# A transformer layer pair on one core: normalized context by way of memory, maxima folded into the queries, and a new order

## What is computed

```python
# layer 0: keys and values are the first 112 context rows
Q, K, V = relu(x @ Wq.T + bq), relu(c @ Wk.T + bk), relu(c @ Wv.T + bv)
out = softmax(causal_and_key_mask(Q @ K.T / 4)) @ V          # per head
x = gamma * norm(out * query_mask + x) + beta
# layer 1
q, k, v = split(layernorm(x) @ sa_wqkv)
r = x + merge(softmax(causal(q @ k.T / 16)) @ v) @ sa_wproj
k2, v2 = split(layernorm(ctx) @ ed_wkv)                      # all 375 rows
r = r + merge(softmax((layernorm(r) @ ed_wq) @ k2.T / 16) @ v2) @ ed_wproj
result = r + relu(layernorm(x) @ ff_w1) @ ff_w2
```

## Time and profile before

| | |
|---|---|
| median of 3 runs | 367.59 us (367.25 to 367.86) |
| profiled execution, its own time | 367.8 us |
| its span | 366.1 us |
| granted TensorE clock | 0.999 of full |
| DMA | 14.12 MB in 5300 packets |

### The profile page before, as it was taken

How to read it: one execution, slowest core, us unless ns; L and a number is a source line. 1 busy time by engine, 2 the same in 40 slices (tenths; PEclk the granted TensorE clock), 3 DMA queues, 4 the chain that set the end, 5 groups by cost and what they waited for, 6 DMA issues and landing times.

```text
span 366.1 us, 9692 instructions
## 1 busy us (share of the span) xinstructions
PE 348.3 (95%) x4144; PEld 262.9 (72%) x4144; DVE 224.6 (61%) x563; ACT 170.9 (47%) x299; POOL 52.2 (14%) x67
## 2 busy tenths in 40 slices
PE   8988999999999999999999999999999999999996
PEld 4656788777965678876876776766987768675674
DVE  4789998436668746567945758556944464264412
ACT  2267652650664255673444062763453643614350
POOL 2023331041022010122100041130100031000000
PEclk9999999999999999999999999999999999999999
DMA  7759202000000002000000200000000000000000
GB/s 200 218 192 376 69 23 92 2 2 0 27 0 2 2 7 81 27 14 15 3 2 8 79 2 14 2 2 14 1 4 0 2 2 2 15 2 13 4 2 25
DMA packets 5300, 14.12 MB, mean 39 GB/s; under 512 B 689, under 2 KB 2982, under 8 KB 5002
## 3 DMA queue, kind: packets, MB, share of 16 engines
q1 hardware_dynamic: 4970, 13.42, 11.1%
q10 hardware_dynamic: 288, 0.09, 0.1%
HBM read 12.59 MB, written 0.92 MB: 37 GB/s over the span
## 4 chain that ended last, share of the span: by engine, by line
PE 76%; DVE 13%; DMA 5%; ACT 2%; issue 2%; SPq 1%; POOL 0%; DVEq 0%
PE ring L501 35%; PE ring L743 8%; PE acc L647 8%; PE ring L757 5%; PE ring L622 5%; DVE negmax L1031 4%; PE ring L602 4%; PE ring L596 3%; DMA xh<-in_keys 3%; PE ring L634 2%; DVE negmax L1010 2%; PE ring L666 2%; PE ring L614 2%; DMA w_qk<-in_w_qk 1%; PE ring L708 1%
## 5 line engine op out<-in xcount | busy, mean ns | idle before, releaser
L1031 DVE TENSOR_REDUCE negmax<-ring 112x2 f32<-112x750 f32 x64 | 57.0, 936 | 23.7 <-PE ring L743 23.0
L856 ACT ACTIVATE exps<-ring 125x896 f32<-125x896 f32 x48 | 41.4, 914 | 39.5 <-PE ring L757 39.2
L1248 POOL TENSOR_SCALAR_AFFINE_SELECT exps<-exps 112x896 f32<-112x896 f32 x32 | 30.8, 987 | 118.9 <-ACT exps L856 118.9
L1010 DVE TENSOR_REDUCE negmax<-ring 112x8 f32<-112x896 f32 x32 | 33.4, 1085 | 22.1 <-PE ring L602 22.0
L743 PE MATMUL ring<-k,q 32*112 32x376 f32 x256 | 38.5, 518 | 1.2 <-ACT exps L856 0.5
L647 PE MATMUL acc<-exps,v 125*17 125x112 f32 (+1 forms) x1280 | 38.9, 261 | 0.2
L647 PEld LDWEIGHTS acc<-exps,v 125*17 125x17 f32 (+1 forms) x1280 | 28.1, 97 | 12.9 <-issue 10.3
L856 ACT ACTIVATE exps<-ring,pad 112x896 f32<-112x896 f32 x32 | 30.5, 1004 | 10.7 <-PE ring L634 10.6
L501 PE MATMUL ring<-w_b,h 128*112 128x256 f32 x128 | 29.3, 382 | 0.0
L501 PEld LDWEIGHTS ring<-w_b,h 128*112 128x112 f32 x128 | 22.1, 177 | 5.8 <-issue 1.1
L501 PE MATMUL ring<-n,w_b 128*128 128x224 f32 x128 | 25.7, 357 | 0.2
(11 more groups left out here) (139 smaller groups left out, 547.2 us busy)
## 6 DMA issues: line engine op xcount, KB each, us to landing
c_nat<-in_ctx SPq DMA_DIRECT2D x4, 750.0 KB
w_b<-in_w_b SPq DMA_DIRECT2D x1, 2304.0 KB, 13.4
xk_t<-in_xk_t SPq DMA_DIRECT2D x8, 224.0 KB, 4.6
w_a<-in_w_a SPq DMA_DIRECT2D x1, 1280.0 KB, 6.0
xh<-in_keys SPq DMA_DIRECT2D x4, 224.0 KB, 4.1
x_nat<-in_x SPq DMA_DIRECT2D x4, 224.0 KB, 3.3
out<-x SPq DMA_DIRECT2D x8, 112.0 KB, 1.8
rows_sb<-in_row SPq DMA_DIRECT2D x1, 560.0 KB, 7.8
```

The costliest lines, as they stand in the source:

```text
L856: return nc.scalar.activation(exps[0:k, EXP_AT[job], :, :], o[0:k, :, 0:4 * T], ACT.Exp, bias=bias)
L1010: v_max[b].step(nc.vector.tensor_reduce(negmax[0][:, slot(g, b), 2 * m_:2 * m_ + 2, :], o[0:T, :, 0:4 * T].rearrange("p r (j t) -> p r j t ...
L1031: x_max[b].step(nc.vector.tensor_reduce(negmax[1][:, b, 2 * m_:2 * m_ + 2, i], o[0:T, :, 0:S], AX.X, ALU.max, negate=True), g, 2 * i + m_ + 1)
L1248: p_masked[b].step(nc.gpsimd.affine_select(e, e, [[0, 8], [1, T]], ALU.is_ge, 0.0, base=0, channel_multiplier=-1), g, k)
```

## The change

Three things. First, the context comes a second time with features on partitions (`c_feat`); the numbers of each token (deviation and shift, `c_norm`) are written to memory and read back as rows spread over 128 partitions (`c_rows`); GpSimd multiplies and adds. ScalarE's normalizing and TensorE's transposes go. Second, keys too are kept twice with one head of each pair zeroed, and one idle row of the zeroed head holds a 1 in the keys; the maximum goes into that row of the queries (new steps `Q`, `cQ`, on VectorE), so that the product of keys and queries contains the subtraction. The scores less the maxima are then sixteen products of 112 columns. Third, `MIX` is a new string.

```diff
 def p_steps(g):
-    return [("stats", g), ("cnorm", g)] + [(n, g, b) for b in range(G) for n in ("cT", "k2", "v2")]
+    return [("stats", g), ("cnorm", g)] + [("cN", g, b) for b in range(G)] + [(n, g, b) for b in range(G) for n in ("cT", "k2", "v2")]
...
-MIX = ("ALALNNCANDEECDCNPICWNCWDPJEWJICPDDICPJDNDIPIAJPIAAAJCJIHHJDERPCDECEDCJDCDPAIAAKAHIJNAAAPBPBEJABPJIFFIBJICPBFEFPBEBPBBBFN"
+MIX = ("AANCENLPDPECDLCDWANDCDNPIDNJCIJPWICJPWCJEIDPNCDPIPJIJAIPJJAAHCHIDAEDCDCPDPEPCEHIDPJCDCJJIIPEPAJRAIAKANPAHBJBJABIFNIPEBAB"
...
+            def load_context_features(g, b):
+                if g:
+                    sp.wait_ge(*v_ct.at(g - 1, b + 1))
+                sp.dma_start(c_feat[b][:, :, :], c_t_d.rearrange("(c p) t -> p c t", p=128)[:, :, (g * G + b) * S:(g * G + b + 1) * S]).then_inc(c_feat_loaded[b], 16)
+
+            def spread_norm(g):
+
+                sp.wait_ge(*v_cnm.done(g))
+                sp.dma_start(norm_d[g].rearrange("k (n p) -> p k n", p=CH), c_norm[:, :, :], allow_slow_non_contiguous=True).then_inc(norm_stored, 16)
+                if g + 1 < NG:
+                    load_context(g + 1)
+                sp.wait_ge(norm_stored, 16 * g + 16)
+                for b in range(G):
+                    if g:
+                        sp.wait_ge(*p_cn[b].done(g - 1))
+                    sp.dma_start(c_rows[b][:, :, :], norm_d[g][:, b * S:(b + 1) * S].unsqueeze(0).to_broadcast([128, 2, S])).then_inc(c_rows_loaded[b], 16)
...
-            def minus_max(bank, i, k):
+            def shifted(bank, k, keys, queries):
 
                 for c in range(C):
-                    for r in range(R):
-                        rows = slice(32 * r, 32 * r + 32)
-                        nc.tensor.matmul(bank(r)[0:k, 2 * c * T:2 * (c + 1) * T], sel[rows, c:c + 1].to_broadcast([32, k]), maxrows[i][rows, :], start=c == 0, stop=False, skip_group_check=True)
+                    for e in range(2):
+                        for r in range(R):
+                            rows, j = slice(32 * r, 32 * r + 32), 2 * c + e
+                            m = nc.tensor.matmul(bank(r)[0:k, j * T:(j + 1) * T], keys(rows, c, e), queries(rows, c, e), start=j == 0, stop=True, skip_group_check=True)
+                            if j == 3 and r % 2:
+                                end(m)
...
-            def context_normed(g):
-                act.wait_ge(*v_cnm.done(g))
-                for i in range(G * NCH):
-                    b, ch = divmod(i, NCH)
-                    a_cn.step(nc.scalar.activation(c_nat[:, b, ch, :], c_nat[:, b, ch, :], ACT.Identity, bias=c_nm[:, i:i + 1], scale=c_rstd[:, i:i + 1]), g, i + 1)
...
             def context_hi(g, b):
                 if g or b:
                     is_filled(act, ("v2", g, b - 1) if b else ("v2", g - 1, G - 1))
-                a_ct.step(nc.scalar.activation(ct[:, HI, :, 0:S], is_filled(act, ("cT", g, b))[:, :, 0:S], ACT.Copy), g, b + 1)
+                act.wait_ge(*p_cn[b].done(g))
+                a_ct.step(nc.scalar.activation(ct[:, HI, :, 0:S], c_feat[b][:, :, :], ACT.Copy), g, b + 1)
...
+            def less_maximum(signal_, g, k, job, q, b):
+
+                o = is_filled(dve, job)[:, 0, 0:T].unsqueeze(1).to_broadcast([128, C, T])
+                for e in range(2):
+                    signal_.step(nc.vector.scalar_tensor_tensor(q[:, :, b, e, :], o, vec[:, EO + 1 - e:EO + 2 - e], q[:, :, b, e, :], ALU.mult, ALU.add), g, 2 * k + e - 1)
...
+            def context_normed(g, b):
+                pool.wait_ge(c_feat_loaded[b], 16 * g + 16)
+                pool.wait_ge(c_rows_loaded[b], 16 * g + 16)
+                p_cn[b].step(nc.gpsimd.tensor_tensor(c_feat[b][:, :, :], c_feat[b][:, :, :], c_rows[b][:, 0, :].unsqueeze(1).to_broadcast([128, C, S]), ALU.mult), g, 1)
+                pool.wait_ge(*p_cn[b].last(g))
+                p_cn[b].step(nc.gpsimd.tensor_tensor(c_feat[b][:, :, :], c_feat[b][:, :, :], c_rows[b][:, 1, :].unsqueeze(1).to_broadcast([128, C, S]), ALU.add), g, 2)
```

More of the change, by code:

```diff
@@ L451, in _ @@
             sp.dma_start(unsplit.rearrange("p c u -> p (c u)"), w_d["kv2"]).then_inc(kv_loaded, 16)
+            for b in range(G):
+                load_context_features(0, b)
             def general():
@@ L624, in self_max_rows @@
             def self_max_rows(g, l, b):
[L625 removed]
+                max_rows(("M", g, l, b), slot(g, b), v_max[b].at(g, 4) if l else v_seen[b].done(g))
             def self_shifted(g, l, b):
                 bank = quad(("X", g, l, b))
[L629 to L637 removed]
+                pe.wait_ge(*v_less[b].at(g, 2 * l + 2))
@@ L639, in add_values @@
+                shifted(bank, T, lambda rows, c, e: kf[g % 2][rows, c, b, e, :], lambda rows, c, e: qf[g % 2][rows, c, b, e, :])
             def add_values(s, vals, job, opens):
@@ L747, in cross_max_rows @@
             def cross_max_rows(g, b):
-                max_rows(("cM", g, b), x_spread[b].done(g))
+                max_rows(("cM", g, b), 4 + b, x_max[b].done(g))
             def cross_shifted(g, b, ch):
                 bank = quad(("cX", g, b, ch))
-                pe.wait_ge(*c_m[b].done(g))
-                minus_max(bank, 4 + b, CH)
-                for c in range(C):
-                    for r in range(R):
-                        rows = slice(32 * r, 32 * r + 32)
-                        m = nc.tensor.matmul(bank(r)[0:CH, 2 * c * T:2 * (c + 1) * T], k2[g % 2][rows, b, c, ch * CH:(ch + 1) * CH],
-                                             q2[g % 2][rows, c, b, :, :].rearrange("p e t -> p (e t)"), start=False, stop=True, skip_group_check=True)
-                        if c == C - 1 and r % 2:
-                            end(m)
+                pe.wait_ge(*x_less[b].done(g))
+                shifted(bank, CH, lambda rows, c, e: k2[g % 2][rows, b, c, e, ch * CH:(ch + 1) * CH], lambda rows, c, e: q2[g % 2][rows, c, b, e, :])
             def cross_sum(g, b, ch):
@@ L1220, in _ @@
             dve.wait_ge(prep_dve, PREP_DVE)
-            run({"rows": rows_summed, "flag": flag, "general": general, "f": add_hidden, "split": weights_lo, "keys": keys, "masks": masks, "late": late_masks, "v0": values0, "S": self_maxima, "M": self_spread, "O": self_out, "dev": deviation0, "norm": norm1,
+            run({"rows": rows_summed, "flag": flag, "general": general, "f": add_hidden, "split": weights_lo, "keys": keys, "masks": masks, "late": late_masks, "v0": values0, "S": self_maxima, "M": seen, "Q": self_less, "O": self_out, "dev": deviation0, "norm": norm1,
                  "v1": values1, "proj": residual1, "norm2": norm2,
-                 "stats": context_statistics, "cnorm": context_shift, "cT": context_lo, "v2": values2, "cS": cross_maxima, "cM": cross_spread,
+                 "stats": context_statistics, "cnorm": context_shift, "cT": context_lo, "v2": values2, "cS": cross_maxima, "cQ": cross_less,
                  "cO": lambda g, b: out_normed(("cO", g, b), x_o[b], 1, g, b, b), "y": result})
```

211 lines of the change are left out of this document (92 added, 119 removed).

## The result

The changed kernel takes 394.26 us (median of 4, 393.57 to 397.71), the kernel before 367.73: ratio 1.0735, 95% interval 1.0686 to 1.0784. Forecast were 381.5 us, 364 to 400.

A forecast was written before the change was run, and what follows sets the result against it. VectorE's order was taken to bound the start, TensorE the rest. Span 366.1 + 14 (start) + 6.8 (second pair) + 8.8 (third) - 16.7 (TensorE's savings) + 1 (waits) = 380.0; median 1.5 above: 381.5 us, range 364 to 400.

The forecast's parts named there:

- TensorE's savings: Work taken off TensorE after the start by cheaper shifted scores, cheaper maxima steps and vanished context transposes: 16.7 us.
- the 7.2 us: Saving on shifted-score steps, X and cX: 0.20 us on each of the 36 after the start.
- 1 us for waits that they add (0 to 5): After the start: allowance for waits from VectorE's and ScalarE's changed work, otherwise taken as covered by TensorE's work.
- a near balance: ScalarE after the start: copies of maxima and context normalizing saved against keys written twice, taken to about cancel.
- The start, 14 us: Total delay in the first pair: 8 us from context statistics going first on VectorE, 6 us from the store.
- The further 6 us: First pair: VectorE's late masks wait for `v_all_ready`, which SyncE raises only after its wait for the store.
- 9.0 + 1.8: The store of the context's numbers to memory: 9.0 us for its pieces plus 1.8 us to land.
- 30 ns a piece: Assumed time of each 4-byte piece of the store, 300 pieces on each of five DMA engines: 9.0 us.
- (b): Second pair: the 23.1 us chain from shift to normalized context outlasts TensorE's work in between; costs 6.8 us.
- (c): Third pair: GpSimd, waiting for the rows, stands ahead of a score's masking and so delays V(2,0,0); costs 8.8 us.
- the second rival: Round trip as forecast, but the engines' order hides it in (b) and (c): 366 to 373 us, chance 0.13.
- 354.5 + 3D: Forecast time in us, with D the time of the store's pieces, for D over 3 us; break-even at 4.4 us.

The follow-up runs named there:

- e1: The new code of the maxima (idle rows, keys written twice) with the context's way and the order of the kernel before: 381.6 us.
- e8: e1 with ScalarE writing the keys only once, both heads' products reading that copy (scores wrong): 370.1 us.
- e4: Changed kernel with each context load and each store of the norm split into two DMAs, partitions 0 to 111 and 112 to 124: 393.2 us.
- e6: Changed kernel with the rows loaded from an input, so that they wait for nothing; the store is still issued: 397.8 us.
- e3: Idle-row maxima in the new order, with the context's way of the kernel before and two steps moved: 405.0 us.
- e9: Changed kernel with the next pair's context load issued behind the rows instead of ahead of them: 398.0 us.
- e7: Changed kernel with GpSimd's two passes cut from 375 columns to 8, most of the context left unnormalized: 384.6 us.
- e12: Changed kernel with GpSimd's passes cut to 8 columns, the next context load behind the rows, and the context load split in two: 374.7 us.
- e10: Kernel before with the context's new way alone, keys written once, old order with a few steps moved and loads reordered: 392.5 us.

## Why the prediction was right, and where not

**TensorE's savings (16.7 us).** The forecast took the shape of the plain scores for all steps. That holds for X, 0.98 us undisturbed where it was 1.15. But 24 of the 40 steps are cX with 125 keys, 1.07 us where it was 1.17 to 1.18:

```profile
254.37 1.14 PE L641 MATMUL ring<-q,k 32*125 32x112 f32 x32
255.44 0.96 PE L661 MATMUL acc<-exps,v 125*17 125x112 f32 x32
```

So the 7.2 us are 24 by 0.11 and 12 by 0.17, 4.7 us, and the savings 14.2. And "1 us for waits that they add (0 to 5)" was the wrong size. I called ScalarE's part "a near balance" and did not follow who waits for the keys: writing them twice costs 11.5 us in the old order (e1 less e8). Without that the idle rows still gain nothing there (e8).

**The start, 14 us.** The context lands at 21.18 (21.2 forecast), and 4.4 us earlier bring 5.3 (e4): right. The further 6 us for the store and `v_all_ready` are wrong: SyncE's wait ended at 33.48 and VectorE idled 2.09 us for it, and e6, where VectorE does not idle there (`x_nat` at 33.72) and the context comes 0.4 us later, has its q1 copy at the same 74.01. In its place stands the new order itself, some 15 us between e1 and e3 without k2. Which of its steps costs them beyond the statistics no run says. The term came out 4.5 us short.

**The store.** 7.4 us where 9.0 + 1.8 were forecast, and both terms were off. 30 ns a piece was too high: alone in flight the pieces take 2.8 us, 9 ns each if 300 of them go one behind the other on each of five engines. The landing was too low, 2.6 us there and 4.9 when split. What the runs support is 6 to 9 us for the store, split or not.

**(b) Second pair, 6.8 us.** 7.77. The place and the mechanism are right, and e9 confirms that the next context ahead of the rows is part of it, 4.6 us (7.5 forecast). That the size came out within 1 us is luck: a chain 3.4 us shorter met an order with less cover than I counted.

**(c) Third pair, 8.8 us.** It did not happen. V(2,0,0) waited for 0.92 us; ScalarE's and VectorE's own work filled the time, the second rival. e4, e6 and e9 each lose 4 to 6 us near that place, by other mechanisms.

**Not in the sum at all.** GpSimd's passes hold VectorE (5.3 us at 261 us; 9.7 is e7's whole gain, the shorter chain included), and TensorE comes back at half clock from its longer idle stretches.

With the terms as the traces have them, the start at 18.5, (b) at 7.8, (c) at 0, 1.4 us of half clock behind (b) (3.29 us from the projection to the next step, 1.88 in e12), 5.3 at 261 and savings of 14.2, the sum is 366.1 + 18.5 + 7.8 + 1.4 + 5.3 - 14.2 + 1 = 385.9, against a span of 392.2. The other 6.3 us I have not placed; the doubled keys are a candidate that no run of the new order tests. So the forecast is right in its sign, at the start and in (b), and owes part of its size to luck: the 8.8 us of (c) that did not come stand about where the start's missing 4.5 and the passes' 5.3 belong. The formula 354.5 + 3D was wrong in its 3: in this kernel neither the first D nor the third counted. The first would with an earlier context: in e4 VectorE idles 5.68 us for SyncE at the start, in e12 3.44.

## What to carry to other kernels

When work moves to GpSimd, price it by what VectorE does in the same microseconds: list VectorE's operations beside it, and what TensorE waits for behind them. When a part doubles the writes of an engine that is 47% busy, follow each write to its reader before calling it hidden. And when one edit gains where its wait was and loses elsewhere (e4, e9), don't drop it; try it again once the next limit is gone (e12).

## What the runs showed of the hardware

- GpSimd's operations on SBUF stop some of VectorE's. L953 (a copy of 112x2) took 1.53 and 1.95 us beside a pass (e9) and 0.15 us alone (e6), L1123 2.13 and 0.47; L1027, which reads PSUM, kept its 0.9 us. The Trainium skill, page "SBUF — State Buffer", section "SBUF: two separate sides", says that the pair of ports that both share is a lock, held for a whole instruction; the trace agrees, one of VectorE's operations per pass.
- 2.07 us of idle at 261 us were followed by 0.58 and 0.56 of the clock in the next two windows, where eight L524 products took 3.35 us instead of 1.78. Full is 2.4 GHz, half 1.2; these windows mix the two. The kernel before never idles for 1 us or more from 20 us on, and its windows read 1.00 up to 350 us.
- 1500 pieces of 4 bytes take 6.1 to 8.6 us from their issue to the end of the wait for them. With nothing else in flight the pieces pass in 2.8 us, in 2.0 when the store is split in two, and the wait ends 2.6 and 4.9 us after the last of them.
- The issue of the load behind such a store takes SyncE 1.87 us; where nothing was stored ahead of it, 0.28.
- TensorE stood for 2.9 to 5.8 us with nothing to wait for that the profile shows while the kernel's own transfers were in flight (e4, e6, e10), the DMA share at 0.9 to 1.1 as the longest three began. What it lacked is not shown. The Trainium skill, page "Runtime: NRT & Kernel Launch", section "Terms", has each engine's instruction memory refilled in blocks of 16 KiB; the page of the profile of e4 agrees in size, 35 packets of q8 for 0.57 MB, and ties none of them to these waits.
